# Edge count and edge sums of the first graph layer: waits, norm statistics, column halves and the order of the sums changed

## The reference

```
src, dst: 10000 edges; xn = layernorm(x)
msg   = relu(xn[src]) + 1e-7
alpha = segment_softmax(msg * t, dst)             # per feature
out   = segment_sum(msg * alpha, dst) + xn
z     = relu(batchnorm(out @ W1 + b1)) @ W2 + b2
x     = x + xn + z
```

## Time and profile before

| | us |
|---|---|
| median of 3 runs | 1828.0 (1827.51 to 1828.8) |
| the profiled execution, its own time | 1827.82 |
| its span | 1826.0 |
| TensorE busy | 1731.0 (95%) |
| VectorE busy | 882.0 (48%) |
| ScalarE busy | 454.2 (25%) |
| GpSimd busy | 688.3 (38%) |

### The profile page before, as it was taken

How to read it: one execution, slowest core, us unless ns; L and a number is a source line. 1 busy time by engine, 2 the same in 40 slices (tenths; PEclk the granted TensorE clock), 3 DMA queues, 4 the chain that set the end, 5 groups by cost and what they waited for, 6 DMA issues and landing times.

```text
span 1826.0 us, 25842 instructions
## 1 busy us (share of the span) xinstructions
PE 1731.0 (95%) x10227; PEld 1590.9 (87%) x10227; DVE 882.0 (48%) x1877; ACT 454.2 (25%) x853; POOL 688.3 (38%) x428
## 2 busy tenths in 40 slices
PE   6799999999998999899899999999999999999999
PEld 6699997898997888889657788888999999998899
DVE  8983234315854549977567653433112131236321
ACT  3543213203122225954303321011011011113210
POOL 1027654553534532032020065433554434342554
PEclk9889999999998999899899999999999999999999
DMA  2001221244111211013110022111212111110222
GB/s 85 1 27 53 77 64 53 61 140 148 52 44 44 62 52 44 1 36 78 72 41 1 1 62 81 51 48 44 61 61 61 44 53 61 44 52 28 63 68 69
DMA packets 42000, 99.85 MB, mean 55 GB/s; under 512 B 10508, under 2 KB 12142, under 8 KB 41894
## 3 DMA queue, kind: packets, MB, share of 16 engines
q1 hardware_dynamic: 37828, 87.87, 15.7%
q10 hardware_dynamic: 4066, 10.46, 1.6%
HBM read 96.39 MB, written 1.92 MB: 54 GB/s over the span
## 4 chain that ended last, share of the span: by engine, by line
PE 77%; DVE 7%; ACT 5%; PEld 3%; issue 2%; POOL 1%; PEldq 0%; DVEq 0%; ACTq 0%; POOLq 0%
PE bank L2301 10%; PE bank L2303 9%; PE bank L2302 9%; PE banks L2301 9%; PE banks L2302 8%; PE banks L2303 8%; PE bank L2834 3%; PE banks L2834 3%; PE bank L2909 3%; PE bank L2914 3%; PE banks L2909 2%; PE banks L2914 2%; ACT prob L1092 1%; PE banks L2689 1%; ACT lesser L1093 1%
## 5 line engine op out<-in xcount | busy, mean ns | idle before, releaser
L788 POOL TENSOR_TENSOR w_hi<-raw,ones_r 128x768 fp32r<-128x768 f32 (+1 forms) x192 | 292.9, 1525 | 1078.5 <-PE banks L2303 381.2
L791 POOL TENSOR_TENSOR w_lo<-raw,w_hi 128x768 fp32r<-128x768 f32 (+1 forms) x192 | 370.6, 1930 | 15.1
L2301 PE MATMUL bank<-w_hi,xT_hi 128*125 128x384 f32 (+2 forms) x560 | 189.0, 337 | 2.8 <-issue 1.6
L2303 PE MATMUL bank<-w_hi,xT_lo 128*125 128x384 f32 (+2 forms) x560 | 187.4, 335 | 0.0
L2302 PE MATMUL bank<-w_lo,xT_hi 128*125 128x384 f32 (+2 forms) x560 | 187.1, 334 | 0.0
L2301 PE MATMUL banks<-w_hi,xT_hi 128*125 128x384 f32 (+2 forms) x440 | 151.9, 345 | 0.8 <-issue 0.8
L2302 PE MATMUL banks<-w_lo,xT_hi 128*125 128x384 f32 (+2 forms) x440 | 151.4, 344 | 0.0
L2303 PE MATMUL banks<-w_hi,xT_lo 128*125 128x384 f32 (+2 forms) x440 | 151.3, 344 | 0.0
L2301 PEld LDWEIGHTS bank<-w_hi,xT_hi 128*125 128x125 f32 x560 | 104.6, 187 | 8.0 <-issue 4.2
L2302 PEld LDWEIGHTS bank<-w_lo,xT_hi 128*125 128x125 f32 x560 | 104.7, 187 | 2.4
L2303 PEld LDWEIGHTS bank<-w_hi,xT_lo 128*125 128x125 f32 x560 | 104.5, 187 | 2.5
(11 more groups left out here) (557 smaller groups left out, 3912.0 us busy)
## 6 DMA issues: line engine op xcount, KB each, us to landing
raw<-wa SPq DMA_DIRECT2D x92, 384.0 KB, 3.0
raw<-wc SPq DMA_DIRECT2D x76, 384.0 KB, 3.1
raw<-wb SPq DMA_DIRECT2D x28, 448.0 KB, 3.4
w_rows<-w_in ACTq DMA_DIRECT2D x1, 3072.0 KB, 12.9
bias<-bias_in ACTq DMA_DIRECT2D x6, 384.0 KB
w_first<-w_in ACTq DMA_DIRECT2D x1, 2304.0 KB, 8.4
w_down<-w_down_in SPq DMA_DIRECT2D x8, 288.0 KB, 5.2
w_up<-w_up_in SPq DMA_DIRECT2D x1, 2304.0 KB, 11.4
```

Source lines behind the costliest of these rows:

```text
L788: pool.tensor_tensor(w_hi[:, k, 0:width], raw[:, k, 0:width], ones[:, 0:1].to_broadcast([P, width]), ALU.mult).then_inc(S("unit_high"), 1)
L791: pool.tensor_tensor(w_lo[:, k, 0:width], raw[:, k, 0:width], f(w_hi[:, k, 0:width]), ALU.subtract).then_inc(S("unit_split"), 1)
L2301: pe.matmul(dst, l_hi, r_hi, start=start, stop=False)
L2303: return pe.matmul(dst, l_lo, r_hi, start=False, stop=stop)
```

## The change

- The halves of the destination columns are 312 and 314 wide instead of 314 and 312; buffers keep a width of 314.
- VectorE waits for three constants before the one-hots and for all 25 in the block of span 1, q = 2, where the sign is now computed; TensorE waits for all 25 at the maximum.
- The norm statistics: ScalarE sums each tile of x with an identity and an accumulator, VectorE scales the sums at q = 2, ScalarE squares the centred rows with an accumulator, VectorE takes the variance at q = 5 and the centre at q = 6.
- Behind the last span VectorE settles and adds the whole counts tile by tile (`settle_end`), then forms the last products and `nm_lo`, and adds the fractions last (`fractions_end`). ScalarE's last two `product_high` come ahead of `second_half`.
- TensorE forms the first two groups together: high parts of both denominators, low parts of both, high parts of both numerators, transposes of two node tiles, low parts of both, transposes of three. Banks are planned in that order.
- VectorE's and ScalarE's loops over groups are staggered by one step more, and product and add of a group are a step apart.

The diff, cut where only names of widths change:

```diff
@@ -29,7 +29,8 @@
 NODES, D = 625, 768
 NT, TN = 5, 125
 NP = NODES + 1
-CH = [(0, 314), (314, 312)]
+CH = [(0, 312), (312, 314)]
+WIDE = 314
 KD = D // P
 EDGES = 10000
 ET = EDGES // TN
@@ -243,11 +244,15 @@
             add(label, i, label + "_read", i + 1)
 
     sweep("A", (("g0_maxT", 0, "g0_max_read", 1), ("g0_maxB", 0, "g0_maxB_read", 1)))
-    for j in range(2 * KD):
+    several_from("g0_den", 0, 2, "g0_den_read")
+    several_from("g0_num", 0, 2, "g0_num_read")
+    del closing[-2:]
+    several_from("g0_xT", 0, 4, "g0_xT_copied")
+    closing.extend([("g0_num", 0), ("g0_num", 1)])
+    several_from("g0_xT", 4, 2 * NT - 4, "g0_xT_copied")
+    for j in range(2, 2 * KD):
         add("g0_den", j, "g0_den_read", j + 1)
         add("g0_num", j, "g0_num_read", j + 1)
-        if j == 0:
-            several("g0_xT", 2 * NT, "g0_xT_copied")
     add("g1_deg", 0, "g1_deg_read", 1)
     several("g0_hidden", 24, "g0_activated")
     turned_behind("g0d", "g0_x", "f0")
...
@@ -951,6 +956,14 @@
             fill_bias("g0_bias_full", 0, D)
 
 
+            for n in range(NT):
+                act.wait_ge(*E(f"x_loaded{n}", 16))
+                act.activation(logits[:, n], x[0:TN, n], ACT.Identity, accum_out=stats[0:TN, n:n + 1]
+                               ).then_inc(S("g0_total"), 1)
+            act.wait_ge(*E("g0_mean", 1))
+            for n in range(NT):
+                act.activation(xn[:, n], x[0:TN, n], ACT.Square, bias=stats[0:TN, NT + n:NT + n + 1],
+                               accum_out=stats[0:TN, 2 * NT + n:2 * NT + n + 1]).then_inc(S("g0_squares"), 1)
             root_of_variance("g0")
             act.wait_ge(*E("bn_var", 1))
             act.activation(bn_s, bn_s, ACT.Sqrt).then_inc(S("bn_std"), 1)
@@ -983,9 +996,9 @@
                 if 0 < n < NT - 1:
                     product_high(n - 1)
             counts("A", adj, 2)
-            second_half("A", adj)
             product_high(NT - 2)
             product_high(NT - 1)
+            second_half("A", adj)
 
             act.wait_ge(*E("cols_loaded", 16))
             act.activation(gates[:, :, 0], cols[:, COLS["f0_gate"][0]:COLS["f3_gate"][1]].rearrange(
...
 
-            for j in range(2 * KD + 1):
-                if j == 1:
+            for j in range(2 * KD + 2):
+                if j == 2:
-                if j:
-                    c0, cn = CH[(j - 1) // KD]
-                    act.wait_ge(*E("g0_sum", j))
-                    act.activation(xT_hi[:, (j - 1) % KD, c0:c0 + cn], tmp[:, (j - 1) % 2, 0:cn], ACT.Copy
+                if j >= 2:
+                    i = j - 2
+                    c0, cn = CH[i // KD]
+                    act.wait_ge(*E("g0_sum", i + 1))
+                    act.activation(xT_hi[:, i % KD, c0:c0 + cn], tmp[:, i % 2, 0:cn], ACT.Copy
                                    ).then_inc(S("g0_out_high"), 1)
             act.wait_ge(*E("g1_deg_ready", 1))
             act.activation(dinv[0:TN], dinv[0:TN], ACT.Sqrt).then_inc(S("g1_dinv"), 1)
...
@@ -1464,9 +1478,27 @@
                         if 1 < span and q <= NT:
                             add_parts(label, target, span - 1, q - 1)
                         during(span, q)
-                settle(label, target, SPANS - 1)
+
+            def settle_end(label, target):
+
                 for s in range(NT):
-                    add_parts(label, target, SPANS - 1, s)
+                    i = LASTS + s
+                    dve.wait_ge(*E(label + "_rounded", i + 1))
+                    dve.wait_ge(*E(label + "_fraction", i - 2 * NT + 1))
+                    STT(fraction_parts[:, s], rounded[:, s], -ROUNDER, bank(label, i)[0:TN, 0:HALF],
+                        ALU.add, ALU.subtract).then_inc(S(label + "_settled"), 1)
+                    dve.wait_ge(*E(label + "_whole_added", i - 2 * NT + 1))
+                    STT(target[:, s, 0:HALF], rounded[:, s], -ROUNDER, f(target[:, s, 0:HALF]), ALU.add, ALU.add
+                        ).then_inc(S(label + "_whole_added"), 1)
+
+            def fractions_end(label):
+
+                for s in range(NT):
+                    i = LASTS + s
+                    total = fraction_sums[:, s]
+                    dve.wait_ge(*E(label + "_settled", i + 1))
+                    dve.wait_ge(*E(label + "_fraction", i - 2 * NT + 1))
+                    TT(total, total, fraction_parts[:, s], ALU.add).then_inc(S(label + "_fraction"), 1)
                 dve.wait_ge(*E(label + "_fraction", LASTS))
                 dve.wait_ge(*E(label + "_whole_added", LASTS))
 
...
             link(dve.tensor_copy(edge[:], e_int[0:TN]))
             split_destinations()
-            dve.wait_ge(*E("consts", CONSTS))
+            dve.wait_ge(*E("consts", 3))
             dve.tensor_copy(iota8, idx8[:, 0:8])
             dve.tensor_copy(rel_index, idx8[:, 8:9])
-            TS(sign, is_low, -2.0, 1.0, ALU.mult, ALU.add)
             def messages(span, q):
 
-                if (span, q) == (0, 3):
-                    for n in range(NT):
-                        dve.wait_ge(*E(f"x_loaded{n}", 16))
-                        for c in range(2):
-                            last = node_stats(n, c)
-                    link(last)
-                    for n in range(NT):
-                        last = dve.bn_aggr(moments[0:TN, 2 * n:2 * n + 2], stats[0:TN, 12 * n:12 * n + 12])
-                    link(last)
-                    TS(rstd[0:TN], moments[0:TN].rearrange("p (n k) -> p n k", k=2)[:, :, 1], LN_EPS, None, ALU.add
-                       ).then_inc(S("g0_var"), 1)
+                if (span, q) == (0, 2):
+                    dve.wait_ge(*E("g0_total", NT))
+                    link(TS(moments[0:TN].rearrange("p (n k) -> p n k", k=2)[:, :, 0], stats[0:TN, 0:NT], 1.0 / D, None,
+                            ALU.mult))
+                    TS(stats[0:TN, NT:2 * NT], stats[0:TN, 0:NT], -1.0 / D, None, ALU.mult).then_inc(S("g0_mean"), 1)
+                    dve.wait_ge(*E("consts", CONSTS))
+                    TS(sign, is_low, -2.0, 1.0, ALU.mult, ALU.add)
                     dve.wait_ge(*E("cols_loaded", 16))
                     TS(bn_s, col("bn_var"), 1e-5, None, ALU.add).then_inc(S("bn_var"), 1)
-                elif (span, q) == (0, 4):
+                elif (span, q) == (0, 5):
+                    dve.wait_ge(*E("g0_squares", NT))
+                    TS(rstd[0:TN], stats[0:TN, 2 * NT:3 * NT], 1.0 / D, LN_EPS, ALU.mult, ALU.add
+                       ).then_inc(S("g0_var"), 1)
+                elif (span, q) == (0, 6):
                     dve.wait_ge(*E("scalars_loaded", 32))
                     TS(t_eps[0:TN], t_col[0:TN], 1e-7, None, ALU.mult)
                     dve.wait_ge(*E("g0_std", 1))
@@ -1697,10 +1728,12 @@
                     products(q - 2)
 
             one_hots("A", edge[:, 0], adj, messages)
+            settle_end("A", adj)
             products(NT - 1)
             for n in range(NT):
                 dve.wait_ge(*E("g0_num_high", n + 1))
                 TT(nm_lo[:, n, 0:D], msg[:, n], f(nm_hi[:, n, 0:D]), ALU.subtract).then_inc(S("g0_num_low"), 1)
+            fractions_end("A")
 
...
@@ -1718,24 +1751,30 @@
             dve.wait_ge(*E("g0_num_low", NT))
             dve.memset(xT_full[:, :, NODES:NP], 0.0).then_inc(S("g0_xT_pad"), 1)
             dve.wait_ge(*E("g0_xT_pad", 2))
-            for j in range(2 * KD + 1):
-                if j < 2 * KD:
-                    (c0, cn), ft = CH[j // KD], j % KD
-                    at, T, R = slice(c0, c0 + cn), tmp[:, j % 2, 0:cn], tmp[:, 2 + j % 2, 0:cn]
-                    dve.wait_ge(*E("g0_den_read", j + 1))
-                    link(dve.reciprocal(R, R))
-                    await_group(dve, "g0_num", j)
-                    TT(T, bank("g0_num", j)[:, 0:cn], R, ALU.mult).then_inc(S("g0_num_read"), 1)
-                    dve.wait_ge(*E("g0_num_read", j + 1))
-                    if j == 0:
-                        dve.wait_ge(*E("g0_xT_copied", 2 * NT))
-                    TT(T, T, xT_full[:, ft, at], ALU.add).then_inc(S("g0_sum"), 1)
-                if j >= 1:
-                    i = j - 1
+            for j in range(2 * KD + 2):
+                if j >= 2:
+                    i = j - 2
                     (c0, cn), ft = CH[i // KD], i % KD
                     dve.wait_ge(*E("g0_out_high", i + 1))
                     TT(xT_lo[:, ft, c0:c0 + cn], tmp[:, i % 2, 0:cn], f(xT_hi[:, ft, c0:c0 + cn]), ALU.subtract
                        ).then_inc(S("g0_out_low"), 1)
+                if j < 2 * KD:
+                    cn = CH[j // KD][1]
+                    T, R = tmp[:, j % 2, 0:cn], tmp[:, 2 + j % 2, 0:cn]
+                    dve.wait_ge(*E("g0_den_read", j + 1))
+                    link(dve.reciprocal(R, R))
+                    await_group(dve, "g0_num", j)
+                    if j >= 2:
+                        dve.wait_ge(*E("g0_out_low", j - 1))
+                    TT(T, bank("g0_num", j)[:, 0:cn], R, ALU.mult).then_inc(S("g0_num_read"), 1)
```

(72 more changed lines are left out.)

1 line of the change is left out of this document (removed).

## The result

The changed kernel takes 1835.5 us (median of 7 runs, 1832.8 to 1838.9) against 1829.1 us for the kernel before beside it (7 runs): ratio 1.0037, 95% interval 1.0025 to 1.0049. It is 6.4 us slower. The forecast was 1825.1 us with a range to 1828.8, so the result lies outside it, on the side that was given least weight. The profiled execution of the changed kernel took 1832.8 us, with a span of 1831.1 us, 5.1 us more than the 1826.0 of before.

The account below looks back on a forecast made before the run. TensorE, busy 95% of the span, was taken to bound the kernel, with only the start of its dense stream near 104 us moving the end. Terms -3.7 + 0.8 = -2.9 us from 1828.0 gave 1825.1, range 1822.0 to 1828.8.

Parts of the forecast that it names:

- Steps 1 and 2: First slices: early one-hots save 3.3 us less 0.5 for meeting GpSimd; statistics off VectorE save TensorE 5.75 us.
- Step 3: After the first span's counts: ScalarE's messages are late next, ending at 31.1; TensorE resumes 5.6 us earlier, not 8.55.
- Step 4: Low clock behind TensorE's gap: first maximum at 39.6, gain taken as 3.7 us; then VectorE paces everything to 86 us.
- Step 5: End of count and sums: bank waits, low clock, -0.7 to +1.8 us, taken +0.8; loop loses 0.12 us a turn.
- (a): Clock stays high at both resumptions, or one: -6.1 us, 1821.9; one alone about -4.5; chance 0.28.
- (b): At the early one-hots GpSimd and VectorE strictly take turns: 2.1 us more, 1827.2, or 1828.9 with low clock; chance 0.15 with (d).
- (d): In the norm statistics VectorE waits for ScalarE's totals or squares; size counted inside (b); chance 0.15 together with (b).
- (c): Slower: long low clock after a resumption, in span 1 and at sums: +6.2 us, 1834.2; only sums +2.4; chance 0.07.

Follow-up runs that it names:

- e5_rounding_first: e2_front with three of ScalarE's five messages moved behind its five roundings of the first span's counts; 1822.3 us, ratio 0.9959.
- e2_front: The kernel before with only the early one-hots, the norm statistics on ScalarE and all constants asked for later; 1826.2 us, ratio 0.9978.
- e1_loop: The changed kernel with VectorE's low part of the group two back moved between reciprocal and product; 1830.1 us, ratio 1.0004.
- e9_halves_later: e1_loop with ScalarE reading the first two denominators ahead of its five second halves of the counts; 1826.2 us, ratio 0.9982.
- e7_sums_early: e1_loop with VectorE's five fraction adds and ScalarE's second halves behind the first two reciprocals and first reading of denominators; 1828.3 us, ratio 0.9991.
- e8_same: The kernel before, unchanged, measured and profiled again; 1830.1 us, ratio 1.0002.

## Why the prediction was wrong

**Steps 1 and 2 held.** By the matmul that starts at 32 us in the kernel before, the lead was 8.55 us, as forecast. First one-hot 6.13 (forecast 6.2 to 6.5), first matmul 6.95 (7.3). The 0.5 us set aside for meeting GpSimd's selections did not come: one-hots stretched to 0.42 us at most, and one selection took 0.36 us instead of 0.18. ScalarE's sums ended at 13.0 (14.5), the squares at 20.5 (21.5), and the table load behind them was hidden, as said.

**Step 3 held** to a few tenths: rounding at 31.20 (31.1), TensorE again at 32.28 (32.2). e5_rounding_first shows that the cause was the one named: with the messages behind the roundings, 2.8 us of that gap go.

**Step 4 held** at its first place: the granted clock was 0.54 in the microsecond from 32 and 0.50 in the next (the lower of its two levels, 1.2 GHz), behind TensorE's stop of 3.76 us, and 0.75 from 35 to 36; the first maximum came at 39.67 (39.6). Windows of 1 us, TensorE, changed kernel:

```profile
32.00:33.00 1.00, 0.72 (x3) 0.54 0.00 0
33.00:34.00 1.00, 1.00 (x5) 0.50 0.00 0
35.00:36.00 1.00, 1.00 (x8) 0.75 0.00 0
```

Its last sentence, that VectorE alone paces all to 86 us, was too simple. A low stretch of 6.8 us from 56.0, where the kernel before had 3.4 us from 61.2, came with waits of VectorE for TensorE; the settling began at 83.13, 3.1 us early rather than 4.2.

**Step 5 failed in its last sentence, and its sum for the stream was too small.** Its bank waits are all there: TensorE stopped for ScalarE's denominators, 1.41 us, and twice for VectorE's products, 1.86 and 1.88:

```profile
96.67 0.86 PE L2349 MATMUL bank<-ident,xn 125*128 125x125 f32 x6 [1.41 <-ACT tmp L1030]
99.40 0.65 PE L2349 MATMUL bank<-ident,xn 125*128 125x125 f32 x4 [1.86 <-DVE tmp L1769]
101.92 1.93 PE L2349 MATMUL banks<-ident,xn 125*128 125x125 f32 x8 [1.88 <-DVE tmp L1769]
```

The ten pairs started at 103.51 (101 to 103). From the settling to 140 us the kernel lost 2.3 us (-3.1 to -0.8), and 0.9 more by 144 us, not the +0.8 taken, with low stretches of 6.8 us at 100.4 and 3.4 at 137.9 where one of 3.4 was counted. Not all of that is the new order: e2_front, with the old one, goes from -3.3 at 80 us to -1.7 at 140. By medians e1_loop, the change with its loop mended, stands 3.8 us above e2_front, and e9_halves_later, where ScalarE's other halves no longer stand ahead of its reading of the denominators, takes 3.9 us back, 1.3 of them seen at its first reciprocal. The step had counted these halves at 1 us (99.6, not 98.65).

The step that failed is "its loop loses 0.12 us a turn by taking add and product apart ... so this only keeps VectorE clear". To lose means here that the turn gets shorter, and the 0.12 us was right: an add right behind its product starts 0.52 us after it, in the new order 0.40. But the same edit put the low part right behind the sum on which ScalarE has to work first. That turn is 3.34 + 0.60 = 3.94 us. Over eleven turns the last low part, due about 142 (it comes at 143.0 in e1_loop), comes at 148.7, and the margin by which TensorE trails it was 0.2 us, a figure that stood in the very same sentence. With it fails the opening statement that whatever moves the start of the dense stream moves the end "and nothing else does": the loop moved the end and not that start. From 144 to 149 us the kernel loses 3.1 us (+0.1 to +3.2).

**The sum** of the one trace by its own terms: -3.1 at 83 us (forecast -3.7), +3.2 for the sums (+0.8), +3.1 for the loop (0), and +1.9 behind it, where nothing was forecast and where two executions of one program differ as much: 5.1. By medians, each against the kernel before beside it, the whole is +6.4: the front -3.3, e1_loop +0.5, so 3.8 for the late part with its loop mended, and 5.9 for the loop. The loop is nearly the whole loss; without it the change would still have gained nothing, since the late part gave back what the front had won.

**The rivals.** (a) and (b) did not come, nor (d). (c), the slower one, had the right sign for another reason: low stretches are 87 us in all in the changed kernel's trace and 84 in that of before, and e1_loop, which mends only the loop and has 87 us of low clock too, is 5.4 us faster. (The range up to 1828.8 also cuts off the end of (b), 1828.9, which it was said to take in.) What was missing is the rival that a moved instruction loses its cover. The prediction costed each edit by what it took away, and for the loop it never wrote down, for one turn, who answers whom and what runs meanwhile.

## What to carry to other kernels

When a loop is taken apart into stages, write one turn down as a list and look at every instruction that waits for another engine: how much work of its own engine lies between the request and the use of the answer? An exchange VectorE, ScalarE, VectorE took 1.0 us from the start of the sum to the start of the low part here; put behind a reciprocal of 2.1 us it costs nothing, put next it costs 0.5 to 0.6 us a turn. And where a consumer trails a producer by 0.2 us, every edit of the producer's loop is an edit of the critical path.

## What the runs showed of the hardware that was not expected

VectorE's adds of two SBUF operands and GpSimd's splits hold each other up. The fraction adds took 0.48 us each alone (0.4 from start to start). In e7_sums_early the three that began beside the splits, from 98.74 on, took 1.75 to 2.13 us, and the two behind the last split 0.47. The other way round, one of GpSimd's own w_hi, at 92.66 in e1_loop, where VectorE was at the five adds, took 3.16 us instead of 1.47. Reciprocals beside the same splits kept their 2.10 us. The Trainium skill (GPSIMD Engine Reference, section Specifications) names this case, VectorE instructions "with two SBUF inputs", beside those in a two-port mode; these rows agree, and the expectation for e7_sums_early had not weighed it. The selections at 6 to 9 us, of 4 or 32 partitions, cost the one-hots 0.04 us at most.

TensorE's low stretches begin at other places in two executions of one program, 27.1 and 25.8, 61.2 and 63.3 us in the profiles of before and e8_same, and one may last 3.4 us here and 6.8 there. Its slow start differs as well: the last tile that takes 1.31 us starts at 11.64 in the one and at 14.23 in the other, though both profiles give a granted clock of 1.00 for 14 to 15 us, so the pace there is read from starts. The spans differ by 1.9 us: 1.0 us of it is there at 16 us and 1.7 at 32. In all, the low stretches are as long in both (84 us): where they fall matters, not only their sum.
